# An audio tower on one core: equal chunks of 32 batches, more buffers, and the gate product as a step of its own

## The reference

```python
h = einsum('bnp,dp->bnd', patches, W) + b
# attn(x), x = layernorm(h):
z, xv, Bm, Cm, dt_in = split(rmsnorm(x) @ in_proj_w.T)
dt = softplus(dt_in @ dt_proj_w.T + dt_proj_b)
dA = exp(dt[..., None] * -exp(A_log));  dBx = (dt * x_full) * Bg     # 1024 channels, 16 states
h_i = dA_i * h_(i-1) + dBx_i;  y_i = sum over the 16 states of C_i * h_i
x1 = x + (y + D_skip * x_full) * silu(z) @ out_proj_w.T
attn = x1 + silu(rmsnorm(x1) @ gate_w.T) * (rmsnorm(x1) @ up_w.T) @ down_w.T
h = h + attn
h = h + silu(layernorm(h) @ w_gate.T) * (layernorm(h) @ w_up.T) @ w_down.T
```

## Time and profile before

| | us |
|---|---|
| median of 3 runs | 751.81 (750.53 to 771.94) |
| the profiled execution | 759.4 |
| its span | 757.6 |
| TensorE busy | 629.1 (83%) |
| VectorE busy | 465.0 (61%) |
| GpSimd busy | 462.9 (61%) |
| ScalarE busy | 337.2 (45%) |
| moved by DMA | 150.37 MB, mean 198 GB/s |

### The profile page before, as it was taken

How to read it: one execution, slowest core, us unless ns; L and a number is a source line. 1 busy time by engine, 2 the same in 40 slices (tenths; PEclk the granted TensorE clock), 3 DMA queues, 4 the chain that set the end, 5 groups by cost and what they waited for, 6 DMA issues and landing times.

```text
span 757.6 us, 8215 instructions
## 1 busy us (share of the span) xinstructions
PE 629.1 (83%) x2718; PEld 518.2 (68%) x2718; DVE 465.0 (61%) x587; ACT 337.2 (45%) x636; POOL 462.9 (61%) x252
## 2 busy tenths in 40 slices
PE   5867665979877879678859596879999999899998
PEld 4746543645434667467738475665899999899998
DVE  4278877786879888979978999751322132322132
ACT  3587784468877333222233222212443342543341
POOL 0377864497879976768687877454354454354451
PEclk9998887999988879999969999989999999999999
DMA  8597773699698869997988899952333434133431
GB/s 336 170 249 188 196 216 105 160 262 298 180 276 241 259 177 301 283 303 228 327 258 265 275 301 276 253 143 89 135 116 115 135 117 134 54 114 116 134 111 43
DMA packets 38922, 150.37 MB, mean 198 GB/s; under 512 B 4320, under 2 KB 8288, under 8 KB 38240
## 3 DMA queue, kind: packets, MB, share of 16 engines
q1 hardware_dynamic: 38880, 149.85, 66.8%
HBM read 145.24 MB, written 4.59 MB: 198 GB/s over the span
## 4 chain that ended last, share of the span: by engine, by line
PE 41%; DVE 25%; DMA 14%; ACT 9%; issue 7%; POOL 2%; SPq 1%; DVEq 0%; ACTq 0%; POOLq 0%
PE work L921 29%; PE da L921 11%; DVE da L720 10%; DMA cb<-c_rows 7%; DVE hs L731 6%; DMA wraw<-w_stream 4%; DMA bb<-b_rows 3%; ACT da L525 3%; PE work L931 1%; ACT L502 1%; DVE gated_n L846 1%; DVE ysum L745 1%; DVE pair L821 1%; DVE pair L841 1%; DVE ysum L747 1%
## 5 line engine op out<-in xcount | busy, mean ns | idle before, releaser
L436 POOL TENSOR_TENSOR hs<-dtx,bb 128x1000 f32<-128x1000 f32 (+1 forms) x64 | 172.0, 2688 | 87.3 <-DMA bb<-b_rows 73.7
L720 DVE TENSOR_TENSOR_SCAN da<-da,hs 128x390 f32<-128x390 f32 (+1 forms) x192 | 194.2, 1042 | 34.7 <-ACT da L525 12.3
L525 ACT ACTIVATE da<-dt,a_neg 128x225 f32<-128x225 f32 (+1 forms) x256 | 115.9, 492 | 178.1 <-DVE hs L731 177.9
L415 POOL TENSOR_TENSOR ws<-wraw,ws 128x1024 fp32r<-128x1024 f32 x40 | 102.2, 2554 | 112.2 <-ACT ws L533 112.2
L921 PE MATMUL work<-sq,wraw 128*128 128x250 f32 x512 | 120.1, 394 | 28.6 <-DMA wraw<-w_stream 16.8
L921 PE MATMUL work<-hn,win 128*128 128x250 f32 (+1 forms) x336 | 113.8, 492 | 31.5 <-DVE hn L788 11.8
L921 PEld LDWEIGHTS work<-sq,wraw 128*128 128x128 f32 x512 | 100.8, 200 | 48.2 <-DMA wraw<-w_stream 19.9
L921 PEld LDWEIGHTS work<-hn,win 128*128 128x128 f32 x336 | 71.4, 218 | 68.0 <-issue 32.7
L731 DVE TENSOR_TENSOR hs<-da,cb 128x780 f32<-128x780 f32 (+1 forms) x96 | 99.9, 1040 | 16.0 <-DMA cb<-c_rows 12.3
L533 ACT CAST ws<-wraw 128x1024 fp32r<-128x1024 f32 x48 | 50.3, 1049 | 93.7 <-PE work L921 46.9
L447 POOL TENSOR_TENSOR hs<-hs 128x500 f32<-128x500 f32 (+1 forms) x48 | 72.4, 1508 | 23.8 <-DVE hs L731 23.8
(11 more groups left out here) (105 smaller groups left out, 683.3 us busy)
## 6 DMA issues: line engine op xcount, KB each, us to landing
wraw<-w_stream SPq DMA_DIRECT2D x104, 512.0 KB, 5.0
bb<-b_rows SPq DMA_DIRECT2D x32, 780.0 KB, 12.7
cb<-c_rows SPq DMA_DIRECT2D x32, 780.0 KB, 9.6
bb<-b_rows SPq DMA_DIRECT2D x32, 500.0 KB, 5.9
cb<-c_rows SPq DMA_DIRECT2D x32, 500.0 KB, 5.8
win<-w_in SPq DMA_DIRECT2D x4, 1024.0 KB, 13.3
c_rows<-c_rows SPq DMA_DIRECT2D x8, 195.0 KB, 3.7
win<-w_in SPq DMA_DIRECT2D x1, 1280.0 KB, 7.6
```

The lines of the kernel that those rows point to most:

```text
L415: nc.gpsimd.tensor_tensor(ws[:, k % NW, 1, :], wraw[:, split_loads[k] % NRAW, :], ws[:, k % NW, 0, :].bitcast(F32), ALU.subtract).then_inc ...
L436: nc.gpsimd.tensor_tensor(hs[:, u % NH, 0:NQ * n].rearrange("p (n t) -> p n t", t=n), dtx[:, t % 2, 0:n].unsqueeze(1).to_broadcast([P, NQ, ...
L525: last = nc.scalar.activation(dst, src, ACT.Exp, scale=a_neg[:, j:j + 1])
L720: nc.vector.tensor_tensor_scan(da[:, k % ND, 0:w], da[:, k % ND, 0:w], hs[:, u % NH, p * w:(p + 1) * w], 0.0, ALU.mult, ALU.add).then_inc( ...
```

## The change

Both chunks get 32 batches, 320 columns. Since 640 doesn't fit a bank of 512, chunk 0 takes the four-scan form too, and `recurrence` gives every unit the same six steps. C rows get three buffers and raw weights six; the first weight loads are issued after in_z(1, 2) instead of in_z(1, 0). The gate product `times_gate` is a VectorE step of its own, placed by `spread` ahead of the `gu` step. TensorE does the state sum ahead of all steps of a slot in each unit whose number leaves 1 when divided by 4.

```diff
-CBS = (25, 39)
+CBS = (32, 32)
...
-NH, NB, ND, NC = 4, 3, 4, 2
+NH, NB, ND, NC = 4, 3, 4, 3
...
-NRAW, NW = 4, 3
+NRAW, NW = 6, 3
...
 def recurrence(u):
 
-    if u // UNITS == 0:
-        behind = [("times_c", u - 1, 0)] if u >= 1 else []
-        return [("scan", u, 0)] + behind + [("scan", u, 1)]
-    behind = [("times_c", u - 1, 0)] if u == UNITS else []
-    return [("scan", u, 0)] + behind + [("scan", u, 1), ("times_c", u, 0), ("scan", u, 2), ("scan", u, 3), ("times_c", u, 1)]
+    return [("scan", u, 0), ("scan", u, 1), ("times_c", u, 0), ("scan", u, 2), ("scan", u, 3), ("times_c", u, 1)]
...
+        sb("cb_beyond_hn2", [P, NC * NQ * TM - 2 * KD * TM])
...
-                    full(sp, ("in_z", 1, 0))
+                    full(sp, ("in_z", 1, 2))
...
-                    if s == ("in_z", 1, 0):
+                    if s == ("in_z", 1, 2):
                         for i in range(NRAW):
                             load_w(i)
...
-                        if i == 0:
-                            dve.wait_ge(dt_ready, NCH * KI)
-                        dve.wait_ge(th_done, i + 1)
-                        link(nc.vector.scalar_tensor_tensor(out=gate2[:, 0:n], in0=th[:, i % 2, 0:n], scalar=1.0,
-                                                            in1=bank((s, "gate")), op0=ALU.add, op1=ALU.mult))
-                        dve.sem_inc(free_of((s, "gate")), 1)
+                        freed(dve, (s, "gate"))
                         full(dve, s)
...
+            def times_gate(s):
+
+                i, n = tile_of(s), TS[s[1]]
+                if i == 0:
+                    dve.wait_ge(dt_ready, NCH * KI)
+                dve.wait_ge(th_done, i + 1)
+                nc.vector.scalar_tensor_tensor(out=gate2[:, 0:n], in0=th[:, i % 2, 0:n], scalar=1.0, in1=bank((s, "gate")),
+                                               op0=ALU.add, op1=ALU.mult).then_inc(free_of((s, "gate")), 1)
...
                 for s in steps:
+                    others += [("times_gate", s)] if s[0] == "gu" and not is_split(s) else []
...
-                n = (len(steps) + 1) // 2
+
+                n = 0 if unit is not None and unit % QU == 1 else (len(steps) + 1) // 2
```

More of the change, by code:

```diff
@@ L765, in step @@
                     return
+                if kind == "times_gate":
+                    times_gate(s[1])
+                    return
                 n = TS[c]
```

## The result

The changed kernel ran at 733.53 us in the median of 4 runs (729.65 to 847.92), and at 727.63 (724.61 to 732.87) when it was run again; the kernel before had 756.7 and 758.8 beside them. The ratios are 0.969 [0.960, 0.978] and 0.962 [0.954, 0.970]: **3 to 4% faster**. The forecast of 749 stood against a median of 751.8 then, so it meant 0.4% less; it had the range 722 to 770 around it and held "no change beyond 2%" for likeliest.

What follows compares the result with a forecast made beforehand. TensorE bounds chunk 1 alone; VectorE leads in chunk 0's scans; VectorE, TensorE and DMA are close between. 38.6 + 215 + 45.5 + 246 + 209.6 = 754.7 us span, by factor 0.992 a median of 749, range 722 to 770.

Steps and rivals of the forecast that it cites:

- B: Chunk 0's scans, from the first scan to chunk 1's first scan: 179.9 us before, 215 forecast (VectorE 188 plus waits 27).
- D: Chunk 1's scans over chunk 0's MLPs, until chunk 1's output projection: 244.2 us before, 246 forecast, the bound passing to TensorE.
- the readers: 48 TensorE steps of 16 records in chunk 0's MLPs: 3.40 us each before, 4.34 forecast at 320 columns.
- the weight waits: TensorE's waits for weights during chunk 1's scans over chunk 0's MLPs: 27.3 us before, forecast under 8.
- The first rival: Waits vanish during chunk 0's scans (200 us) and chunk 1's scans over chunk 0's MLPs (236): median 724, chance 0.26.
- The second rival: ScalarE and VectorE wait for each other over decays in chunk 0's scans, 240 us there: median 774, chance 0.12.
- E: Chunk 1 alone, from its first output-projection matmul to the end, TensorE's stretch: 248.8 us before, 209.6 forecast.
- the fixed reading: With chunk 1 alone, the 0.0152 us atop a split matmul record stays fixed: 0.1485 us at 320 columns, 33.6 us less.
- the scaled one: With chunk 1 alone, the 0.0152 us atop a split matmul record scales with columns: 0.1458 us, 36.7 us less.
- The third rival: Weight loads bound TensorE with chunk 1 alone, a record staying at 0.1777 us: median 782, chance 0.05.
- C: From chunk 1's first scan to chunk 0's first second-norm matmul: 50.6 us before, 45.5 forecast through lighter four-scan units.
- A: Prologue up to the first scan: 34.1 us before, 38.6 forecast, +4.5 for 82 TensorE records with 70 more columns.

Runs made afterwards that it cites:

- equal chunks alone: Changed kernel with 32 and 32 batches kept, but C buffers, weight buffers, gate step, state sum and weight-stream start as before: 727.08 us, 0.963 of the kernel before.
- short readers: Changed kernel with the 48 readers of chunk 0's MLPs run over 250 of the 320 columns, the rest left out: 720.41 us, 0.951 of the kernel before.
- 28/36: Changed kernel with 28 batches in chunk 0 and 36 in chunk 1: 754.72 us, 0.992; with the chunks alone changed, 744.15 us, 0.980 of the kernel before.
- 30/34: Changed kernel with 30 batches in chunk 0 and 34 in chunk 1: 742.24 us, 0.977 of the kernel before.

## Why the prediction was right or wrong

**Direction and size.** The time fell by 3 to 4% where the forecast had 0.4%. The measured times lie inside its range, and "no change beyond 2%", which it held likeliest, did not come. Its own sign of being wrong did: B and D together are 448.6 us, 12.4 under the 461 that it allowed to be off by 12. Of its other signs the readers (4.33 us for 4.34), the weight waits (none) and the clock in D (0.96) held; the DMA share in D is 0.85 for 0.79. The first rival (724, "waits vanish") gave the total, though not by its own split: its D (236) was still too long and its B (200) too short, so that it met the total is luck.

**B: right, and partly by luck.** VectorE 188 forecast, 185.7 measured; a unit 4.8 forecast, 4.7 measured; waits 27 forecast, 33.4 measured. Their kinds were wrong. POOL's input term no longer holds VectorE up (11.9 before), the state sum neither (7.9), softplus neither. What came is a wait for C rows, 22.5 us, of which the earlier trace rows show nothing. It is there with the old chunks in four-scan form too (26.8 us in that run's groups), so it goes with the form, not with 320 columns: the first product of a unit now comes after two scans of its own unit instead of behind the next unit's first scan, so C rows are wanted earlier (the order of steps says so; no run shifts it). The third C buffer doesn't cure it: with two, the wait is 17.8 us in the new order and 13.2 in "equal chunks alone". The difference lies near the end of B, in VectorE's timeline of the changed kernel:

```profile
245.98 0.82 DVE L728 TENSOR_TENSOR hs<-da,cb 128x640 f32<-128x640 f32 x1 [7.96 <-DMA cb<-c_rows]
```

From 219.8 us on SyncE issues the first six weight blocks there, 3 MB at once, and the C loads of 215 to 250 us take 13.0 us to land in the median. With four blocks begun at the same step they take 9.5 and the longest wait is 4.5; with four begun at in_z(1, 0) it is 2.5. "Starting the weight stream at a later step costs nothing" is thus not borne out in B, though the medians don't show the price. The second rival did not happen: VectorE's wait for decays is 12.4 us, 8.8 of it ahead of the first scan.

**E: right.** 209.6 forecast, 205.5 measured. The chain in time of the changed kernel:

```profile
563.95 7.04 PE work L926 x48
```

7.04/48 = 0.1467 us, between the fixed reading (0.1485) and the scaled one (0.1458); over 1152 records that is 2.1 of the 4.1 us missed. With 0.1640 at 360, 0.1560 at 340 and 0.1373 at 300 columns (7.87, 7.49 and 6.59 us for 48), the amount on top of columns/2.4 GHz is 15.2, 14.0, 14.3, 13.3 and 12.3 ns from 390 down to 300. So it shrinks a little, and I chose the wrong one of two near readings. It is not 2.5 ns at any width. The third rival, the record held at 0.1777 by weight loads, is refuted by every one of these runs. The weight-load row is busy 191.8 of 205.5 us in E (93%) where it was 227.5 of 248.8 (91%), so the share of that row didn't show the room that was there. The Trainium skill ("Perfetto Trace Analysis", section "Identifying the Most-Contended Engine") names that share, beside one other, as a measure of how close TensorE is to its limit; this trace doesn't agree.

**D: wrong, the step that failed.** "D = 208 + 22 + 9 + 7 = 246". Measured: readers 768 x 0.2705 = 207.7, as forecast; the chains 5.2 + 12.6 = 17.8 for 22; waits for gated products and banks 0 for 9; a clock below full about 4.7 for 7 (the records after a chain: 37.70 and 36.24 for 34.62). I named the new bound, "So the bound passes to TensorE", and then still charged it 9 us of waits that belong to an engine that is not the bound, and some 6 us too much for chains and clock. (The sentence "the gain in waits (about 36 us)" misreads the sum beside it, which keeps 9 of the 36 and takes 17 off the clock's part.) Before, TensorE waited because the recurrence and its transfers held it back. Once its own work was longer than theirs, the waits had nothing to come from. By the step's own words "six weight buffers instead of four and three for C instead of two take most of the first" I also gave the cure to the wrong part: the buffers, with the new orders, do remove those waits, and it gains nothing clear (1.004); the columns alone remove them too, and it gains 4%. The short readers show for gated products that the waits come back with the slack; for weights with four buffers no run parts TensorE's new place from the 10% fewer bytes.

A second number in D was also off, without harm to the sum. I priced the DMA engines at 193 us by 294 GB/s and so left them 53 us behind. With TensorE's work taken away they stood at 217 us, 0.94 busy. A rate worked out from a stretch with a share of 0.89 did not hold at 0.94.

**C: open in size.** 45.5 forecast, 41.4 measured; but against the 45.8 and 43.6 of the other profiles with 390 columns the drop is 4.4 or 2.2 where 5.1 was forecast. I took VectorE's lighter units for the price, where the row of C says POOL: busy 46.1 of 50.6 before, 40.8 of 41.4 after. "About 17% less" of 50.6, which I wrote beside it, is 42.

**A: probably right.** +4.5 forecast, +1.5 measured against 34.1. Against the 31.2 and 30.5 us of the other profiles with 250 columns it is +4.3 and +5.1, so the base was off and not the price.

**The gate step and the early state sum** were priced at nothing in D, and nothing is what they bring: the two kernels at 32/32 without them and with them differ by less than 1%. At 28/36 they cost about 10 us: 0.992 [0.986, 0.999] with them and 0.980 [0.973, 0.986] without, and each of the four executions with them (752.8 us and up) is slower than each of the four without (748.6 at most). The profiles put it not in D (241.3 with, 242.6 without) but in B (202.5 for 198.0; VectorE waits 28.3 us for C rows there for 16.3, 7.3 of it once, behind the first weight blocks) and in E (233.2 for 229.7, 2.0 of it the wait for the last `z`). No run parts the buffers from the orders there.

**The four-scan form** was the right thing to fear in B. It costs 17 us and takes the kernel to 1.020 by itself; the split has to earn that back before it wins.

## What to carry to other kernels

When a stretch's bound passes to another engine, drop that engine's old waits from its new time, except those of chains it is itself part of; keep them only if the other side is within their size, and work out the other side's finish as a second time. With two sides that trade work, the best split is where both finish together: read who waits for whom at the hand-over (here TensorE for the last `z`, 4.3 us at 30/34, 0.4 at 32/32), since near that point the wait and the lower clock behind it come on top of the columns. Extra buffers can remove the waits of an engine with slack and leave the end where it was, and the larger first load of a deeper queue can hold up what stands behind it.

## What was not expected of the hardware

- A weight block of 512 KB took 11.4 us to land in D before and 5.7 after, for a moved total of 64.1 and 57.6 MB. With the short readers it took 10.5 at 57.4 MB: the same bytes queue twice as long when TensorE is not the last.
- The DMA engines moved 263 to 285 GB/s per full busy share in D at shares of 0.93 to 0.95, 294 at 0.89 before the change, and 293 to 299 in the runs at 0.77 to 0.85. Starting the rows 32 bytes off a 256-byte boundary left the time as it was (286 at 0.87).
- VectorE operations of the same size take very different times beside POOL's work: 0.49 us for `z` (L747) in D, 1.36 us for the same line with `yg` in B, 1.27 for softplus (L821). It moves about from run to run: the product that makes `z` took 1.44 us at 390 columns in D before the change and 0.86 in "equal chunks alone". No run here shows why.
